# Expert lists of a capacity-routed layer: fewer steps from the search to the lists, token weights stored during the search, gathers three experts ahead

## What is computed

```python
scores = (x_flat @ Wg.T).T                        # 8 experts x 4096 tokens
top_vals, token_idx = jax.lax.top_k(scores, 512)  # each expert takes 512 tokens
token_w = jax.nn.softmax(top_vals, axis=-1)
xg = x_flat[token_idx]
h = silu(xg @ W1[e].T) * (xg @ W3[e].T)           # hidden 256
y = (h @ W2[e].T) * token_w[..., None]
out = zeros.at[token_idx].add(y)                  # a token can be taken by several experts
```

## Time and profile before

| | us |
|---|---|
| median of 3 runs (lowest, highest) | 711.26 (710.67, 712.9) |
| the profiled execution | 710.23 |
| its span, first to last instruction | 708.4 |
| busy: PE, DVE, ACT, POOL | 510.0, 425.5, 332.7, 313.6 |
| search | about 94 to 130 |
| search's end to the first gather | about 130 to 144.6 |
| tile loop, first gather to the sums' load | 144.6 to 253.8 |

### The profile page before, as it was taken

How to read it: one execution, slowest core, us unless ns; L and a number is a source line. 1 busy time by engine, 2 the same in 40 slices (tenths; PEclk the granted TensorE clock), 3 DMA queues, 4 the chain that set the end, 5 groups by cost and what they waited for, 6 DMA issues and landing times.

```text
span 708.4 us, 13478 instructions
## 1 busy us (share of the span) xinstructions
PE 510.0 (72%) x3830; PEld 373.5 (53%) x3832; DVE 425.5 (60%) x1784; ACT 332.7 (47%) x690; POOL 313.6 (44%) x329
## 2 busy tenths in 40 slices
PE   1759520278868508777899996059999999999934
PEld 1457100245545304333433433049999999999921
DVE  4789668835412237898527778874445455455447
ACT  3815510034323104455446773156666666666616
POOL 3514300057878732343001221126776766767535
PEclk9966755569978857899999998569999999999967
DMA  7401263022333351100000100021111111111155
GB/s 190 132 0 44 81 269 148 3 41 40 39 47 42 34 174 31 31 15 1 1 1 16 31 24 23 15 29 42 50 49 45 49 48 45 49 45 49 39 198 172
DMA packets 47735, 42.22 MB, mean 60 GB/s; under 512 B 15345, under 2 KB 41834, under 8 KB 47178
## 3 DMA queue, kind: packets, MB, share of 16 engines
q1 hardware_dynamic: 35770, 25.48, 11.5%
q0 software_dynamic: 10816, 15.82, 10.6%
q10 hardware_dynamic: 1104, 0.39, 0.2%
HBM read 26.23 MB, written 15.30 MB: 59 GB/s over the span
## 4 chain that ended last, share of the span: by engine, by line
PE 48%; DVE 24%; issue 10%; ACT 7%; DMA 5%; POOL 5%; ACTq 1%; DVEq 0%; POOLq 0%; SPq 0%
PE bank L1888 18%; PE bank L1909 9%; DVE st L1262 3%; PE bank L1699 3%; POOL sum_dram L676 3%; ACT arena L916 2%; PE bank L1744 2%; PE bank L1800 2%; PE bank L1734 2%; DVE st L992 2%; DVE mv L1267 2%; POOL arena L664 1%; PE bank L1833 1%; PE bank L1898 1%; DVE hit L1106 1%
## 5 line engine op out<-in xcount | busy, mean ns | idle before, releaser
L1888 PE MATMUL bank<-arena 128*128 128x128 f32 x1136 | 140.4, 277 | 0.4 <-ACT arena L967 0.4
L1888 PEld LDWEIGHTS bank<-arena 128*128 128x128 f32 x1136 | 134.2, 194 | 0.7 <-ACT arena L967 0.7
L690 POOL TENSOR_TENSOR rstd<-ve,mhalf 128x4 f32<-128x4 f32 x40 | 48.7, 1218 | 162.1 <-DVE ve L1270 116.0
L1523 DVE TENSOR_TENSOR arena<-arena,bank 128x512 f32<-128x512 f32 x71 | 48.8, 688 | 81.8 <-PE bank L1888 81.8
L744 POOL DMA_INDIRECT y_dram<-arena,sidx x71 | 70.1, 987 | 44.3 <-DVE arena L1528 41.0
L953 ACT ACTIVATE arena<-wgu 128x1024 f32 x71 | 75.0, 1058 | 26.6 <-PE bank L1888 26.2
L736 POOL DMA_INDIRECT arena<-x3row_dram,gidx x71 | 69.0, 972 | 36.7 <-issue 20.7
L1909 PE MATMUL bank<-w,arena 128*128 x568 | 75.1, 275 | 0.0
L1909 PEld LDWEIGHTS bank<-w,arena 128*128 128x128 f32 x568 | 69.1, 192 | 0.2 <-issue 0.2
L959 ACT ACTIVATE arena<-bank 128x512 f32<-128x512 f32 x71 | 42.4, 597 | 42.6 <-PE bank L1888 42.6
L676 POOL DMA_INDIRECT sum_dram<-arena,idx x32 | 50.7, 1586 | 15.2 <-issue 7.9
(11 more groups left out here) (324 smaller groups left out, 1018.7 us busy)
## 6 DMA issues: line engine op xcount, KB each, us to landing
wgu<-in_wgu SPq DMA_DIRECT2D x1, 4096.0 KB, 12.2
wgu<-y_dram SPq DMA_DIRECT2D x8, 512.0 KB, 6.3
X<-in_x SPq DMA_DIRECT2D x8, 256.0 KB, 5.6
sum_dram<-zero POOLq DMA_DIRECT2D x8, 256.0 KB, 4.2
x1row_dram<-row SPq DMA_DIRECT2D x8, 256.0 KB, 2.4
w<-in_w SPq DMA_DIRECT2D x1, 2048.0 KB, 17.3
acc<-sum_dram SPq DMA_DIRECT2D x8, 256.0 KB, 2.9
w<-in_wd SPq DMA_DIRECT2D x1, 2048.0 KB, 9.3
```

Of the source, the lines that this page charges most:

```text
L690: nc.gpsimd.tensor_tensor(out, ve[:, u], mhalf[:, 0:J], ALU.pow).then_inc(done, 1)
L1523: nc.vector.tensor_tensor(gl[:, m.pair], sgl[:, m.pair], bank[3 + m.pair][:], ALU.mult).then_inc(f_gated, 1)
L1888: last = nc.tensor.matmul(bank[first + m.pair][:, h * P:(h + 1) * P], wnow[:, m.pair, at_:at_ + P], xrT[:, m.ring], start=True, stop=True)
```

## The change

Slots come from two independent scans over `sel` and `eq`, with both sums from PE made beside them; slots are numbered from -7.5 (that is, minus 8.5) on, and 0 marks a token that is not taken. The high digit is made by adding and subtracting 1.5 x 2^27, which rounds to a multiple of 16; the low digit is what is left; the values compared with are constants `iota_lo`, `iota_hi`. The exponentials are turned by PE in round 5 of the search, copied by ACT and stored without their divisor; the divisor's reciprocal is a second scalar of the weighting step. ACT makes one Silu of a single column behind that copy. Three lists are made ahead of the tile loop; POOL gathers experts 0 to 2 first, and then one expert at a time; gathers from number 8 on also wait until the tile eight before has been turned. Expert 0's rows are stored without an add.

```diff
@@ -52,6 +52,8 @@
 LEAD = 1
 ROWS = D + E0
 YW = D + E1
+MID = 8.5
+TO_16 = 1.5 * 2.0 ** 27
 XG = 12
 BY_DVE = 4
 
@@ -175,8 +177,8 @@
         tile128_b = sb("tile128_b", [P, T], BF16)
         blk_b = sb("blk_b", [P, P], BF16)
         tri_b = sb("tri_b", [P, P], BF16)
-        qi = sb("qi", [P, 2, SEG], I32)
-        qf = sb("qf", [P, 2, SEG])
+        iota_lo = sb("iota_lo", [P, 16, 2], BF16)
+        iota_hi = sb("iota_hi", [P, 32, 2], BF16)
         slots = sb("slots", [P, SEG])
         cand = sb("cand", [P, 2, 4], U32)
         step = sb("step", [P, 1], U32)
@@ -661,6 +663,8 @@
                     n = 4 * e + k
                     if n >= XG:
                         pool.wait_ge(c_yw, LEAD + n - XG + 1)
+                    if n >= 8:
+                        pool.wait_ge(c_xtps, LEAD + n - 8 + 1)
                     nc.gpsimd.indirect_dma_start(xg[:, n % XG], None, x1row_dram,
                                                  bass.IndirectOffsetOnAxis(ap=idx[:, e, k:k + 1].bitcast(U32), axis=0)
                                                  ).then_inc(c_xg[n % 8], 16)
@@ -673,17 +677,20 @@
                 for k in range(4):
                     n = 4 * e + k
                     pool.wait_ge(c_yw, LEAD + n + 1)
-                    nc.gpsimd.indirect_dma_start(sum_dram, bass.IndirectOffsetOnAxis(ap=idx[:, e, k:k + 1].bitcast(U32),
-                                                                                     axis=0),
-                                                 yw[:, n % 8], None, compute_op=ALU.add).then_inc(c_acc[k], 16)
-            gather0(0)
-            gather0(1)
+                    rows = bass.IndirectOffsetOnAxis(ap=idx[:, e, k:k + 1].bitcast(U32), axis=0)
+                    if e:
+                        nc.gpsimd.indirect_dma_start(sum_dram, rows, yw[:, n % 8], None,
+                                                     compute_op=ALU.add).then_inc(c_acc[k], 16)
+                    else:
+                        nc.gpsimd.indirect_dma_start(sum_dram, rows, yw[:, n % 8], None).then_inc(c_acc[k], 16)
+            for e in range(3):
+                gather0(e)
             for e in range(E0):
                 add0(e)
-                if e + 2 < E0:
-                    gather0(e + 2, range(0 if e == 0 else 2, 4))
                 if e + 3 < E0:
-                    gather0(e + 3, range(2))
+                    gather0(e + 3, range(4 if e + 3 < E0 - 1 else 2))
+                elif e + 3 == E0:
+                    gather0(E0 - 1, range(2, 4))
 
             def power(out, u, wait, n, done):
                 pool.wait_ge(wait, LEAD + n)
@@ -825,6 +832,12 @@
             nc.scalar.activation(base[:, 2:3], bank[4][:, 0:1], ACT.Copy, scale=-1.0).then_inc(c_ex, 1)
             act.wait_ge(c_ex, LEAD + 1)
             nc.scalar.activation(ex[:], srch[:], ACT.Exp, bias=base[:, 2:3]).then_inc(c_ex, 1)
+            act.wait_ge(c_mxps, LEAD + 3)
+            for h in range(2):
+                last = nc.scalar.activation(wtok[:].rearrange("p (s h) e -> p h e s", h=2)[:, h],
+                                            bank[5][:, h * P:(h + 1) * P].rearrange("p (e s) -> p e s", e=E0), ACT.Copy)
+            last.then_inc(c_wtok, 1)
+            nc.scalar.activation(cg[:, 1:2], ones[:, 0:1], ACT.Silu)
 
 
             def places(e):
@@ -833,6 +846,7 @@
                 nc.scalar.activation(oneB[:, e % 2, :, 0:16], hotB[:, e % 2], ACT.Copy, scale=pcol[:, 0:1]).then_inc(c_valp, 1)
             places(0)
             places(1)
+            places(2)
             act.wait_ge(r_wr, LEAD + 4)
             nc.scalar.activation(wo[:, P:], bank[0][:, E1:2 * E1], ACT.Copy).then_inc(r_wr, 1)
 
@@ -851,8 +865,8 @@
                     if not early(o, 2):
                         act.wait_ge(c_y, LEAD + o.n - 1)
                     nc.scalar.activation(gT[:, o.pair], bank[4 + o.pair][:, 0:H0], ACT.Copy).then_inc(c_gt, 1)
-                if m and m.n % 2 == 0 and m.n // 2 < E0 - 2:
-                    places(2 + m.n // 2)
+                if m and m.n % 2 == 0 and m.n // 2 < E0 - 3:
+                    places(3 + m.n // 2)
             straight(T, move0, 1, 1)
 
             def normalise(out, src, b):
@@ -1108,6 +1122,8 @@
             nc.vector.tensor_copy(iota_x[:], iota_t[:].unsqueeze(2).to_broadcast([P, P, 2]))
             nc.vector.tensor_copy(tile128_b[:], tile128[:])
             nc.vector.tensor_copy(tri_b[:], tri[:])
+            nc.vector.tensor_scalar(iota_lo[:], iota_t[:, 0:16].unsqueeze(2).to_broadcast([P, 16, 2]), 1.0 - MID, None, ALU.add)
+            nc.vector.tensor_scalar(iota_hi[:], iota_t[:, 0:32].unsqueeze(2).to_broadcast([P, 32, 2]), 16.0, None, ALU.mult)
             nc.vector.tensor_copy(blk_b[:], blk[:]).then_inc(c_cnt, 1)
             ch.mark(nc.vector.memset(step[:], 0))
             ch.wait()
@@ -1157,48 +1173,38 @@
             nc.vector.tensor_scalar(eq[:], srch[:], thr, None, ALU.is_equal, ALU.add,
                                     accum_out=cgb[:, 1:2]).then_inc(c_post, 1)
             dve.wait_ge(c_post, LEAD + 1)
-            nc.vector.tensor_tensor_scan(rank[:], onesW[:], eq[:], 0.0, ALU.mult, ALU.add)
+            nc.vector.tensor_tensor_scan(rank[:], onesW[:], sel[:], 0.0, ALU.mult, ALU.add)
+            ch.mark(nc.vector.tensor_tensor_scan(hit[:], onesW[:], eq[:], 0.0, ALU.mult, ALU.add))
             dve.wait_ge(c_postps, LEAD + 1)
-            ch.mark(nc.vector.tensor_scalar(base[:, 0:1], bank[6][:, 0:1], -1.0, float(CAP), ALU.mult, ALU.add))
+            ch.mark(nc.vector.tensor_scalar(base[:, 0:2], bank[6][:, 0:2], -MID, None, ALU.add))
             ch.wait()
-            ch.mark(nc.vector.scalar_tensor_tensor(rank[:], rank[:], base[:, 0:1], eq[:], ALU.is_le, ALU.mult))
+
+
+            ch.mark(nc.vector.scalar_tensor_tensor(hit[:], hit[:], base[:, 1:2], eq[:], ALU.add, ALU.mult))
+            nc.vector.scalar_tensor_tensor(rank[:], rank[:], base[:, 0:1], sel[:], ALU.add, ALU.mult)
             ch.wait()
-            ch.mark(nc.vector.tensor_tensor(sel[:], sel[:], rank[:], ALU.add))
+            ch.mark(nc.vector.scalar_tensor_tensor(hit[:], hit[:], CAP - MID, hit[:], ALU.is_le, ALU.mult))
             ch.wait()
-            nc.vector.tensor_tensor_scan(rank[:], onesW[:], sel[:], 0.0, ALU.mult, ALU.add).then_inc(c_post, 1)
+            nc.vector.tensor_tensor(slots[:], rank[:], hit[:], ALU.add).then_inc(c_q, 1)
+
+            dve.wait_ge(c_q, LEAD + 1)
             dve.wait_ge(c_ex, LEAD + 2)
-            nc.vector.tensor_tensor(ex[:], ex[:], sel[:], ALU.mult)
-            dve.wait_ge(c_postps, LEAD + 2)
-            ch.mark(nc.vector.tensor_copy(base[:, 3:4], bank[6][:, 2:3]))
-            ch.wait()
-            nc.vector.scalar_tensor_tensor(slots[:], rank[:], base[:, 3:4], sel[:], ALU.add, ALU.mult).then_inc(c_q, 1)
-
-            ch.mark(nc.vector.tensor_reduce(cg[:, 0:1], ex[:], AX.X, ALU.add))
+            ch.mark(nc.vector.scalar_tensor_tensor(rank[:], slots[:], 0.0, ex[:], ALU.not_equal, ALU.mult, accum_out=cg[:, 0:1]))
             ch.wait()
             nc.vector.tensor_scalar(wst[:, 1], emask[:], cg[:, 0:1], None, ALU.mult).then_inc(c_mx, 1)
             dve.wait_ge(c_abps, LEAD + 1)
-            ch.mark(nc.vector.tensor_scalar(qi[:, 0], bank[2][:, 0:SEG], -1.0, None, ALU.add))
+
+            turned = bank[2][:, 0:SEG].rearrange("p (h n) -> p h n", h=2)
+            low, high = (digit[:, k].rearrange("p e s h -> p h (e s)") for k in range(2))
+            ch.mark(nc.vector.tensor_scalar(high, turned, TO_16, TO_16, ALU.add, ALU.subtract))
             ch.wait()
-            ch.mark(nc.vector.tensor_scalar(qi[:, 1], qi[:, 0], 4, None, ALU.arith_shift_right))
+            ch.mark(nc.vector.tensor_tensor(low, turned, high, ALU.subtract))
             ch.wait()
-            ch.mark(nc.vector.tensor_scalar(qi[:, 0], qi[:, 0], 15, None, ALU.bitwise_and))
-            ch.wait()
-            ch.mark(nc.vector.tensor_copy(digit.rearrange("p k e s h -> p k h (e s)"),
-                                          qi[:].rearrange("p k (h n) -> p k h n", h=2)))
-            ch.wait()
-
-            def token_weights():
-                dve.wait_ge(c_mxps, LEAD + 3)
-                ch.mark(nc.vector.reciprocal(wst[:, 2], bank[6][:, 8:16]))
-                ch.wait()
-                nc.vector.tensor_tensor(wtok[:].rearrange("p (s h) e -> p h e s", h=2),
-                                        bank[5][:, 0:2 * P].rearrange("p (h e s) -> p h e s", h=2, e=E0),
-                                        wst[:, 2].unsqueeze(1).unsqueeze(3).to_broadcast([P, 2, E0, 16]), ALU.mult
-                                        ).then_inc(c_wtok, 1)
 
             def compare(out, which, e, n):
                 return nc.vector.tensor_tensor(out, digit[:, which, e].unsqueeze(2).to_broadcast([P, 16, n, 2]),
-                                               iota_x[:, 0:n].unsqueeze(1).to_broadcast([P, 16, n, 2]), ALU.is_equal)
```

(46 more changed lines are left out.)

## The result

The changed kernel takes 703.75 us (median of four runs, 702.11 to 704.9), the kernel before took 710.96 beside it; the ratio is 0.9871, with a 95% interval of 0.983 to 0.9911. The profiled execution took 702.11 us with a span of 700.3, 8.1 us less than before.

A forecast was written before the change was run, and what follows sets the result against it. POOL's issuing was taken to bound the layer; 4.05 (start) + 2.7 (order) + 2.4 (plain stores) = 9.15 us, 9.4 counted at tile 3's store, 9.3 taken, giving 702.0 us, range 699.6 to 704.4.

The forecast's parts named there:

- POOL's issuing bounds the layer: First expert layer, first gather to last adding store: POOL needs 3.2 us a tile, the PE, ACT and DVE loop 2.8.
- Start: Before the gathers: wait for the weights' store goes, list 0 comes 1.56 us earlier, gather 0 4.05 us earlier, at 140.5.
- the step that took 0.27 us from a release to POOL's start: At gather 0: POOL starts 0.27 us after what releases it, so list 0 at 140.25 gives gather 0 at 140.5.
- Order: POOL's queue: twelve gathers ahead of the first store instead of eight; 1.2 of 3.9 us of waiting remain, 2.7 gained.
- Plain stores: Expert 0's four stores on POOL cost 0.99 instead of 1.59 us each, 2.4 us gained.
- Weights: Token weights made in round 5 of the search: their 4.55 us store has over 20 us in hand before 141.
- Tail: POOL's last stores: expert 7's adds still wait for expert 6's to land, 2.54 us, unchanged.
- The first tiles did start earlier: Rival at tile loop entry: first tiles start no earlier, tile 0 entering PE at 147.3; 6.3 us gained, 705.0 us; chance 0.08.
- the store was cheaper: Rival at expert 0's stores: plain store costs what the add costs, 1.3 us less gain, 703.3 us; chance 0.07.
- tile 3 was a wait: Rival at the fourth store: tile 3 is no wait at all, 1.2 us more gain, 700.8 us; no separate chance given.
- PE did not stay at the low clock: Rival in the tile loop: PE stays at low clock and becomes the bound, 4.7 us a tile, up to 717; chance 0.06.
- The rule: Gathers 0 to 2 beside list 2: DVE and GpSimd shut each other out, near 702.3 us; costed at nothing.

The follow-up runs named there:

- the added DMA: Changed kernel plus one indirect DMA of row 0 on POOL ahead of gather 0; first scan behind the search to load of the sums 112.75 us, against 113.06.
- expert 7 gathered early: Changed kernel with all four gathers of expert 7 issued ahead of expert 5's stores; first scan to load of the sums 115.03 us, against 113.06.
- DVE quiet: Changed kernel with DVE waiting for gather 0 to land before making list 2; first scan to load of the sums 116.61 us, against 113.06.
- the second pair: Kernel before and changed kernel, both unedited, measured once more; first scan to load of the sums 122.50 and 113.20 us, ratio 0.9874.
- the weights behind the search: Changed kernel with weights made and stored behind the search again, with divisor, no early Silu; first scan to load of the sums 114.51 us, ratio 0.9878.

## Why the prediction was right

- **POOL's issuing bounds the layer.** Shown: the dearer stores are paid in full (2.57 us), and so is the idle time that three experts ahead fill (5.35).
- **Start.** List 0 came 1.67 us earlier (forecast 1.56), gather 0 only 3.57 by the scan (forecast 4.05): the step that took 0.27 us from a release to POOL's start failed, since the first indirect DMA took 0.86. Gather 0 was also 0.5 us longer.
- **Order.** That lateness cost almost nothing, because the forecast had 1.2 us of waiting for tile 3's row at the fourth store. POOL came 1.0 us later than forecast and waited 0.17 instead. That two lags were swallowed by one wait is luck; where the added DMA took both from gather 0, the stretch was 0.3 us shorter. The fourth store began 29.42 us behind the scan; the forecast's 160.7 is 29.4. The row came 3.12 us earlier, as forecast (3.1), though by another way: tile 0 was 2.8 us earlier (forecast 2.65), and tile 1, 3.1 us earlier, was still held by its gather, which the forecast had ruled out. The product that list 2's chain was expected to end in, the router's, did set tile 0.
- **Plain stores.** 0.98 us, forecast 0.99.
- **Weights.** Their store took 7.7 us, not 4.55, beside the weight loads, and had landed by 117.3, 23 us ahead of need.
- **Tail.** 2.55 us, unchanged, for the reason given: expert 7's stores wait for expert 6's to land, as the kernel with expert 7 gathered early shows.
- **Rivals.** The first tiles did start earlier; the store was cheaper; tile 3 was a wait, if a short one. PE did not stay at the low clock: the granted clock was 0.50 up to 148 us as in the kernel before, and 1.00 in the third window, as there:

```profile
131.00:148.00 17.00, 9.53 (x116) 6.87 (x117) 11.68 (x38) 2.90 (x6) 5.36 (x5) 0.50 0.07 18
148.00:166.00 18.00, 16.66 (x149) 10.91 (x148) 10.37 (x29) 9.46 (x26) 13.57 (x15) 0.92 0.20 55
166.00:190.00 24.00, 21.99 (x183) 15.12 (x182) 11.84 (x41) 10.50 (x33) 19.43 (x16) 1.00 0.33 44
```

- **The rule was dismissed on the wrong pair.** The forecast held the Trainium skill's lock between DVE and GpSimd (SBUF — State Buffer, "SBUF: two separate sides") against one pair of rows that began 0.02 us apart, found that the trace does not agree and costed the overlap at nothing. That section states the lock for two SBUF inputs only against a GpSimd operation that reads SBUF, and the waiting descriptors for DVE's two-port mode. In the pair it was the compare that stretched: 0.74 us, where others take 0.68. The same trace of the kernel before has a pair that speaks the other way, a compare 0.37 us ahead of an adding store that took 1.76 us, where the longest of the other three first stores took 1.63:

```profile
157.91 0.68 DVE L1200 TENSOR_TENSOR arena<-sel,yn 128x1024 bf16<-128x1024 bf16 x1
...
158.28 1.76 POOL L676 DMA_INDIRECT sum_dram<-arena,idx  x1 [0.65 <-DVE arena L1250]
```

  In the changed kernel gather 0 lost 0.5 us beside list 2's compare, as the kernel with DVE quiet shows. What that alone cost the stretch was not measured; the wait for tile 3's row took most of POOL's lateness.

The total of 703.75 lies 1.75 us above the forecast 702.0, though the stretch gained what was forecast. The profiled execution is 1.2 us above its forecast 700.9: 0.42 in the search and 0.92 behind the load, less 0.14 in the stretch; and the median of the runs lies 1.6 us above that execution, where 1.0 was taken. The difference of the medians is 7.2 us here and 9.8 in the second pair (715.67 and 705.91): the total cannot confirm a sum of 9.3, the stretch does.

## What to carry to other kernels

When a queue that issues DMAs is the bound, count its instructions and its idle time apart: reordering so that it hardly waits for its first results was worth more here (5.35 us) than the cheaper instruction (2.57) or the shorter way to its start (1.31 and 1.45). A lag that lies ahead of a wait vanishes in it, so a sum can come out right with wrong terms; check the terms at the point where the wait ends. And measure a gain of one per cent on a stretch with fixed ends, not on a total whose other parts move by half of it (4.5 us) from one profile of a kernel to the next.

## What was not expected of the hardware

**A long DVE compare holds up an indirect DMA that begins behind it, and not one that began before.** The compare of 128x1024 bf16 takes 0.68 us. Pairs from DVE's and POOL's timelines, first of the kernel with the added DMA (compare 0.10 and 0.15 us ahead):

```profile
150.72 0.68 DVE L1213 TENSOR_TENSOR arena<-sel,iota_hi 128x1024 bf16<-128x1024 bf16 x1
...
150.82 1.40 POOL L676 DMA_INDIRECT arena<-x1row_dram,idx  x1 [0.30 <-issue]
...
154.87 0.68 DVE L1213 TENSOR_TENSOR arena<-sel,iota_hi 128x1024 bf16<-128x1024 bf16 x1
...
155.02 1.35 POOL L676 DMA_INDIRECT arena<-x1row_dram,idx  x1 [0.30 <-issue]
```

then of the changed kernel (0.04 us ahead, 0.02 ahead, 0.57 behind the gather at 154.59, and 0.13 behind the store at 161.13 shown above; the row at 154.50 is DVE's gating product):

```profile
141.38 0.67 DVE L1205 TENSOR_TENSOR arena<-sel,iota_hi 128x1024 bf16<-128x1024 bf16 x1
141.42 1.58 POOL L668 DMA_INDIRECT arena<-x1row_dram,idx  x1 [45.39 <-DVE idx L1233]
...
150.82 0.74 DVE L1205 TENSOR_TENSOR arena<-sel,iota_hi 128x1024 bf16<-128x1024 bf16 x1
150.84 0.95 POOL L668 DMA_INDIRECT arena<-x1row_dram,idx  x1 [0.30 <-issue]
...
154.50 0.42 DVE L1256 TENSOR_TENSOR arena<-arena,bank 128x256 f32<-128x256 f32 x1 [0.71 <-ACT arena L862]
154.59 0.95 POOL L668 DMA_INDIRECT arena<-x1row_dram,idx  x1 [0.30 <-issue]
...
155.16 0.68 DVE L1205 TENSOR_TENSOR arena<-sel,iota_hi 128x1024 bf16<-128x1024 bf16 x1
...
161.26 0.68 DVE L1205 TENSOR_TENSOR arena<-sel,iota_hi 128x1024 bf16<-128x1024 bf16 x1
```

With the compare ahead by 0.04 to 0.48 us the DMA takes as much longer as is left of the compare, less about 0.13 us: 0.63 left, 0.49 more than the 1.09 of a first gather; 0.58 left, 0.45 more, and 0.53 left, 0.40 more, than the usual 0.95. Within 0.02 us the compare takes 0.74 and the DMA nothing more; with the DMA ahead neither changes. No pair in the twelve profiles goes against this, with stores as with gathers. The gating product, which reads one of its two inputs from a PE bank, does not do it: it began 0.09 us ahead of the gather at 154.59, which took its 0.95, and wherever it began 0.05 to 0.24 us ahead, in all twelve profiles, the DMA took its usual time.

The Trainium skill's lock (the section named above) is for DVE operations with two SBUF inputs or in a two-port mode, and keeps out whichever of the two begins later. The runs agree with it where the compare began first. They do not agree with the later one being kept out for the whole instruction: the compare that began 0.13 us behind a store of 0.97 us took its usual 0.68. They show the order of the two, not the port.

**The first indirect DMA of the layer begins 0.85 us behind its release where DVE releases it**, by a list or the slots (0.85 to 0.87 us, whichever edit). Where the landing of the weights' store releases it, in the kernel before and with the weights behind the search, it begins 0.27 us behind, as a later one does behind a list (gather 0 behind the added DMA). What the 0.6 us is was not settled.
